# Routing rows of a mixture of experts into a region per expert, batch by batch, with gathered outputs

## The reference

```python
shared = mean over 2 shared experts of gelu(x @ sW1 + sb1) @ sW2 + sb2
gates = xf @ rW + rb                       # 8 experts, 2048 tokens
topk_vals, topk_idx = top_k(gates, 2)
topk_probs = softmax(topk_vals)
h = gelu(xf @ W1[e] + b1[e])               # 128 -> 512
y = h @ W2[e] + b2[e]                      # 512 -> 128
moe = sum over the token's two experts of prob * y
x = layernorm(x + shared + moe)
```

## Time and profile before

| | |
|---|---|
| median of 3 runs | 782.09 us (780.53 to 788.21) |
| span of the profiled execution | 786.9 us |
| PE busy | 566.9 us (72%) |
| DVE busy | 363.1 us (46%) |
| ACT busy | 338.1 us (43%) |
| POOL busy | 251.2 us (32%) |
| moved by DMA | 51.60 MB, mean 66 GB/s |
| mean granted TensorE clock | 0.824 of full speed |

### The profile page before, as it was taken

One profiled execution on the slowest core, in us unless ns is written; L12 is line 12 of the kernel. 1 busy time (PEld: TensorE's weight loads), 2 busy tenths in 40 slices (PEclk: granted clock), 3 DMA queues, 4 the chain that ended last, 5 costly groups with the idle time before them and its releaser, 6 DMA issues.

```text
span 786.9 us, 10406 instructions
## 1 busy us (share of the span) xinstructions
PE 566.9 (72%) x3665; PEld 404.0 (51%) x3665; DVE 363.1 (46%) x1067; ACT 338.1 (43%) x565; POOL 251.2 (32%) x296
## 2 busy tenths in 40 slices
PE   2654552678788869878699882996987696987770
PEld 2213431455355633656436752765874675776660
DVE  4869279616673465645624571226321240133113
ACT  1186574565737556654475140330322242322220
POOL 3204047202351254311613147113322437033231
PEclk9955665689897989987589996999878788969895
DMA  4400000395000000000000102532161402656632
GB/s 125 147 1 1 1 1 0 82 170 195 1 1 1 15 1 0 1 1 1 1 0 1 55 14 69 154 102 67 39 188 43 135 21 100 190 143 182 200 94 80
DMA packets 37763, 51.60 MB, mean 66 GB/s; under 512 B 7097, under 2 KB 27362, under 8 KB 37442
## 3 DMA queue, kind: packets, MB, share of 16 engines
q1 hardware_dynamic: 35218, 45.82, 20.9%
q0 software_dynamic: 2496, 5.15, 1.8%
HBM read 41.28 MB, written 13.86 MB: 70 GB/s over the span
## 4 chain that ended last, share of the span: by engine, by line
PE 44%; DVE 23%; POOL 7%; DMA 7%; ACT 7%; issue 7%; SPq 5%; POOLq 0%; DVEq 0%; ACTq 0%
SPq L427 5%; PE ring_s L850 4%; PE bank_d L760 4%; PE bank_o L880 3%; PE bank_m L682 3%; PE ring_s L652 3%; PE ring_u L747 3%; PE bank_o L866 3%; PE ring_s L844 2%; DMA token_pairs<-y_blk,x_blk 2%; PE bank_o L669 2%; DMA x_blk<-expert_rows 2%; POOL expert_rows L1150 2%; PE bank_r L546 2%; PE ring_u L739 2%
## 5 line engine op out<-in xcount | busy, mean ns | idle before, releaser
L958 ACT ACTIVATE probs<-ring_s 128x512 f32<-128x512 f32 (+1 forms) x192 | 95.5, 524 | 118.6 <-PE ring_s L652 116.9
L1100 POOL TENSOR_SCALAR_AFFINE_SELECT probs<-probs 128x256 f32<-128x256 f32 (+1 forms) x96 | 51.6, 570 | 178.7 <-ACT probs L964 178.7
L652 PE MATMUL ring_s<-qT,kT 64*128 64x128 bf16 (+3 forms) x256 | 64.2, 350 | 49.4 <-ACT probs L958 37.8
L1013 ACT ACTIVATE g_ring<-ring_s,w_blk 128x128 f32<-128x128 f32 x184 | 52.5, 370 | 104.4 <-PE ring_s L850 95.4
L1161 POOL DMA_INDIRECT token_pairs<-y_blk,x_blk x46 | 45.6, 991 | 143.9 <-DVE y_blk L1672 143.1
L964 ACT ACTIVATE probs<-probs 128x2560 f32<-128x2560 f32 x32 | 74.8, 2337 | 0.8
L652 PEld LDWEIGHTS ring_s<-qT,kT 64*128 64x128 bf16 x256 | 16.4, 97 | 93.4 <-ACT probs L958 58.6
L850 PE MATMUL ring_s<-xT_blk,w_blk 128*128 128x128 f32 x368 | 57.0, 305 | 4.3 <-DVE xT_blk L1665 2.6
L682 PE MATMUL bank_m<-pair_sum,oT 128*128 128x64 f32 x256 | 44.0, 327 | 22.2 <-DVE oT L1467 22.2
L1063 POOL TENSOR_TENSOR rstd<-var_eps,neg_half 128x4 f32<-128x4 f32 x24 | 24.9, 1036 | 100.5 <-DVE var_eps L1394 100.4
L850 PEld LDWEIGHTS ring_s<-xT_blk,w_blk 128*128 128x128 f32 x368 | 53.4, 222 | 6.8 <-issue 4.3
(11 more groups left out here) (356 smaller groups left out, 1076.8 us busy)
## 6 DMA issues: line engine op xcount, KB each, us to landing
w_blk<-expert_pack SPq DMA_DIRECT2D x46, 514.0 KB
expert_pack<-in_L_ffn_W SPq DMA_DIRECT2D x16, 256.0 KB
expert_rows<-blank SPq DMA_DIRECT2D x2, 1560.0 KB, 10.5
x_blk<-expert_rows SPq DMA_DIRECT2D x46, 65.0 KB
y_pair<-token_pairs SPq DMA_DIRECT2D x4, 512.0 KB
x_in<-in_x SPq DMA_DIRECT2D x4, 256.0 KB, 2.9
cosm<-in_c_cos SPq DMA_DIRECT2D x1, 1024.0 KB, 6.8
sin_fwd<-in_c_sin_fwd SPq DMA_DIRECT2D x1, 1024.0 KB, 9.4
```

Of the source, the lines that this page charges most:

```text
L652: last = mm(bank[:, c:c + w], kT[64 * r:64 * r + 64, p // 2, P * j:P * (j + 1)], qT[64 * r:64 * r + 64, p, P * j:SEQ], start=True, stop=True)
L958: f(probs[:, p % 2, BASE[n]:BASE[n] + WIDTH[n]], ring_s[k % 2][:, 0:WIDTH[n]], ACT.Tanh, scale=1.0 / (CAP * float(np.sqrt(np.float32(HD))) ...
L1013: last = f(g_ring[:, s % RING, P * n:P * (n + 1)], ring_s[s % 2][:, P * n:P * (n + 1)], ACT.Gelu, bias=w_blk[:, k % SLOTS, HID + n:HID + n ...
L1100: last = g.affine_select(out=v, in_=v, compare_op=ALU.is_ge, fill=0.0, base=0, pattern=[[0, v.shape[1]], [1, P]], channel_multiplier=-1)
```

## The change

- `rows_dram` is laid out by expert: 1024 rows for each of 8 experts in a group, and 896 rows behind them, all filled with zeros (`zero_rows`, eight rows of 512 B a partition, repeated) from SP right after the input loads.
- A row's place in its expert's region doesn't need the block table, so `rows_of(b)` follows `rank` of each batch, and `scatter(b)` writes that batch's rows straight from x2, 8 indirect DMAs of 128 rows. `copy_rows`, `x_rows` and the two extra columns go.
- The block table now also gives each block's source row (`source`), and afterwards, for each token, the rows of its two outputs in block order (`y_rows`); the weights are kept in `w_sel`.
- `load_block` reads two registers, expert and source row. b2, repeated over the partitions, is part of the pack (64 KB more a block, eight more loads at the start), its own load and the one-row matmul go, and DVE adds it at the eviction.
- SP stores block outputs in block order (`store_block`), before the load that reuses the slot; POOL has no part in the blocks. Once a group's outputs have landed, POOL gathers them per batch with 8 indirect DMAs (`fetch`), two batches ahead of their two powers, and `final` has eight multiply-adds of 128x128 in place of two adds of 128x512.

```diff
+CAPACITY = GB * SEQ
+GROUP_ROWS = NE * CAPACITY + (NE - 1) * P
+ZERO_ROWS = 8
+PACK = HID + HC + HID + D
...
+            sp.wait_ge(blank_ready, 1)
+            for g in range(GROUPS):
+                at = g * GROUP_ROWS
+                load(rows_dram[at:at + NE * CAPACITY, :].rearrange("(p n r) w -> p n (r w)", p=P, r=ZERO_ROWS),
+                     zero_rows[:, :].unsqueeze(1).broadcast_to([P, NE * CAPACITY // (P * ZERO_ROWS), ZERO_ROWS * D]), blanked)
+                load(rows_dram[at + NE * CAPACITY:at + GROUP_ROWS, :].rearrange("(p r) w -> p (r w)", p=P), zero_rows[:, 0:(NE - 1) * D], blanked)
             sp.wait_ge(kij_ready, 1)
...
+                load(pack[e, :, B2_AT:PACK], t["L0_ffn_b2"][e].partition_broadcast(P), ld_pack)
...
-            sp.wait_ge(blank_ready, 1)
-            for g in range(GROUPS):
-                load(rows_dram[g * GROUP_ROWS:(g + 1) * GROUP_ROWS, :].rearrange("(p r) w -> p (r w)", p=P),
-                     blank[:, :, :].rearrange("p r w -> p (r w)"), blanked)
...
                 if k >= SLOTS:
                     sp.wait_ge(u_down, BLOCKS[k - SLOTS] + 1)
+                    sp.wait_ge(y_ready_blk, k - SLOTS + 1)
                 e = sp.value_load(table[0:1, g, q:q + 1], min_val=0, max_val=NE - 1)
                 load(w_blk[:, k % SLOTS, :], pack_dram[bass.ds(e * P, P), :], w_landed[k % SLOTS])
-                load(b2_blk[0:1, k % SLOTS, :], t["L0_ffn_b2"][bass.ds(e, 1), :], w_landed[k % SLOTS])
-                if k >= SLOTS:
-                    sp.wait_ge(y_sent[k % SLOTS], 16 * (k // SLOTS))
-                at = g * GROUP_ROWS + q * P
-                load(x_blk[:, k % SLOTS, :], rows_dram[at:at + P, :], xs_landed[k % SLOTS])
...
+                at = sp.value_load(source[0:1, g, q:q + 1], min_val=0, max_val=GROUPS * GROUP_ROWS - P)
+                load(x_blk[:, k % SLOTS, :], rows_dram[bass.ds(at, P), :], xs_landed[k % SLOTS])
+
+            def store_block(k):
+
+                g, q = divmod(k, NB)
+                sp.wait_ge(y_ready_blk, k + 1)
+                load(y_dram[g][P * q:P * (q + 1), :], y_blk[:, k % SLOTS, :], y_sent[k % SLOTS])
...
+                for q in range(NB + SLOTS):
                     k = g * NB + q
...
+                    if q >= SLOTS:
+                        store_block(k - SLOTS)
+                    if q < NB:
+                        load_block(k)
...
-                        mm(dst, g[:, P * n:P * (n + 1)], w_blk[:, k % SLOTS, HID + HC + P * n:HID + HC + P * (n + 1)], start=(n == 0), stop=False)
-                    last = mm(dst, ones2[0:1, :], b2_blk[0:1, k % SLOTS, :], start=False, stop=True)
+                        last = mm(dst, g[:, P * n:P * (n + 1)], w_blk[:, k % SLOTS, HID + HC + P * n:HID + HC + P * (n + 1)],
+                                  start=(n == 0), stop=(n == HC - 1))
...
-                for j in range(GB * NT):
+                pool.wait_ge(blanked, 32 * (b // GB + 1))
+                pool.wait_ge(rows_ready, b + 1)
+                for j in range(NT):
                     for k in range(2):
...
+            def fetch(b):
+
+                if b % GB == 0:
+                    pool.wait_ge(y_rows_ready, b // GB + 1)
+                    for n in range(SLOTS):
+                        pool.wait_ge(y_sent[n], 16 * len(range(n, (b // GB + 1) * NB, SLOTS)))
+                if b >= 2:
+                    pool.wait_ge(pair_used, b - 1)
+                for j in range(NT):
+                    for k in range(2):
+                        g.indirect_dma_start(out=y_pair[:, b % 2, j, k, :], out_offset=None, in_=y_dram[b // GB],
+                                             in_offset=bass.IndirectOffsetOnAxis(ap=y_rows[:, k, b * NT + j:b * NT + j + 1], axis=0)).then_inc(pair_landed[b % 2], 16)
...
+            for of in range(GROUPS):
+                for b in range(GB * of, GB * (of + 1)):
+                    fetch(b)
+                for b in range(GB):
                     power()
...
+                dve.wait_ge(rank_read, b + 1)
+                rows_of(b)
                 if b % GB == GB - 1:
-                    dve.wait_ge(rank_read, b + 1)
                     block_table(b // GB)
-                    rows_of(b // GB)
...
+                one(tt(ends, ends, start_of[:, :].unsqueeze(1).broadcast_to([P, NB, NE]), ALU.mult))
+                one(v.tensor_reduce(source_of[:, :], ends, AX, ALU.add))
+                one(stt(out=source_of[:, :], in0=index[:, 0:NB], scalar=float(P), in1=source_of[:, :], op0=ALU.mult, op1=ALU.add))
+                op(ts(source[0:1, g, :], source_of[0:1, :], float(g * GROUP_ROWS), None, ALU.add))
                 ts(table[0:1, g, :], expert_of[0:1, :], float(NE - 1), None, ALU.min).then_inc(table_ready, 1)
...
-                ts(y_blk[:, k % SLOTS, :], down_bank(k)[:, 0:D],
-                   x_blk[:, k % SLOTS, D + 1:D + 2], None, ALU.mult).then_inc(y_ready_blk, 1)
+                tt(y_blk[:, k % SLOTS, :], down_bank(k)[:, 0:D], w_blk[:, k % SLOTS, B2_AT:PACK], ALU.add).then_inc(y_ready_blk, 1)
...
-                one(tt(a, a, y_pair[:, b % 2, :, 0, :], ALU.add))
-                tt(a, a, y_pair[:, b % 2, :, 1, :], ALU.add).then_inc(pair_used, 1)
+                dve.wait_ge(pair_landed[b % 2], 16 * 2 * NT * (b // 2 + 1))
+                for k in range(2):
+                    for j in range(NT):
+                        last = stt(out=a[:, j, :], in0=y_pair[:, b % 2, j, k, :], scalar=w_sel[:, k, b * NT + j:b * NT + j + 1],
+                                   in1=a[:, j, :], op0=ALU.mult, op1=ALU.add)
```

More of the change, by code:

```diff
@@ L1049, in _ @@
             op(g.memset(ones2[:, :], 1.0))
[L1050 to L1051 removed]
+            op(g.memset(zero_rows[:, :], 0.0))
+            for e in range(NE):
+                op(g.memset(expert_row[:, e:e + 1], float(e * CAPACITY)))
             then()
@@ L1131, in ff_norm @@
                 g.tensor_tensor(fa[:, :, :], fa[:, :, :], x1[:, b % 2, :, :], ALU.add).then_inc(sum_ready, 1)
-            def copy_rows(b):
-                pool.wait_ge(x2_ready, b + 1)
-                if b >= GB and b % GB == 0:
-                    pool.wait_ge(scattered[b // GB - 1], 16 * 2 * NT * GB)
-                for k in range(2):
-                    last = g.tensor_copy(x_rows[:, k, NT * (b % GB):NT * (b % GB + 1), 0:D], x2[:, b, :].rearrange("p (j d) -> p j d", j=NT))
-                last.then_inc(rows_copied, 1)
```

156 lines of the change are left out of this document (70 added, 86 removed).

## The result

The changed kernel is slower by 0.7%, not faster by 2.6%: 786.94 us (median of 19 runs, 778.93 to 803.15) against 782.39 us for the kernel before beside it (19 runs, 774.52 to 803.76). The ratio is 1.0072, 95% interval [1.0038, 1.0106], within the 1% that the prediction called no change. Some executions of either kernel take over 1.5% longer than its fastest; the ratios and intervals here leave those out, the medians don't. The prediction was 761.9 with a range of 748 to 777.

A forecast was written before the change was run, and what follows sets the result against it. No engine was full, so hand-overs between engines set the end. Terms -0.5 + 4.7 - 14.0 + 1.0 - 12.5 - 13.0 + 14.1 = -20.2 us took the median 782.09 to 761.9, range 748 to 777.

The forecast's parts named there:

- Zero fill (1): Start: the fill grows to 9.3 MB, some 34 us, hidden behind SP's 122.5 us wait for the kernel taps.
- x_in (2): Expert pack at the start: x_in of batch 2 lands 5 us earlier to 8 later; -0.5 us, upper end +8.
- Batch 0 alone (3): Batch 0's routing: eight scatters on POOL delay the power queued behind them; +4.7 us, range 0 to 10.
- Batch 1 alone (4): Batch 1's routing: only eight scatters ahead of POOL's power, PE's 14.02 us idle won; -14.0 us, gain 10.1 to 15.5.
- Batch 2 and group 0's blocks (5, 6): Batch 2's scatters and row work +1.0 us; of group 0's blocks, -5.4 near 560 to 589 and -5.0 after 605.
- stays in the sum: DVE's accumulate at 666.37, idle 16.37 us without a known releaser, left unchanged; 6 us put into the range either way.
- have POOL to themselves: Gathers of the first two batches, between scatter(3) and final(0): hidden by some 5 us, 1.264 for each that isn't.
- Batch 3: ... nothing: Batch 3's eight scatters end long before PE needs group 1, so they change nothing.
- Group 1 (6): Group 1's expert blocks: SP's issuing at 3.0 us a block becomes the limit; -13.0 us, gain 0 to 18.
- The end (7): After the last output: 16 gathers, 20.2 us, ahead of two powers, then eight chained steps; +14.1 us, range +10 to +34.
- SP's queue binds more: Rival: SP's queue or the lower clock keeps blocks at 3.5 us, nothing gained in group 1; 780 us, chance 0.13.
- DVE holds POOL up: Rival: batch 0's scatters slowed amid DVE's attention work; +2 us, 764, or +11, 773; chance 0.05.

The follow-up runs named there:

- two_batches: spread with batch 0's scatters held back and issued with batch 1's, 16 in one train; ratio 0.9928 to the kernel before.
- late_rows: spread with DVE's row numbers of batches 0 and 2 some 30 us later, their scatters in two trains of four; 755.66 us, ratio 0.962.
- late_only: The changed kernel with only the later row numbers and scatters of batches 0 and 2, gathers where the change puts them; 777.38 us, ratio 0.9817.
- bias_matmul: spread with the bias added on PE again by a one-row matmul per block and a plain copy as eviction; ratio 0.9954 to the kernel before.
- spread: The changed kernel with the 16 gathers of batches 0 and 1 issued one per block of group 1, their finals later; 768.95 us, ratio 0.9852.
- before_paused: The kernel before with a memset of some 0.94 us waited for after every fourth of group 1's 16 scatters; ratio 1.0017.
- store_on_pool: spread with group 1's 23 output stores issued by POOL as plain DMAs instead of SP; ratio 0.9858 to the kernel before.

## Why the prediction was wrong, step by step

- **Zero fill (1), x_in (2).** Right within what can be told. SP issued the fill from 24 to 42 us, its transfers kept the DMA engines busy until 55, some 30 us where 34 were taken, long before the taps; and PE had no wait for x_in. A loss of 3 us ahead of the first rank matmul would not show.
- **Batch 0 alone (3).** +4.7 predicted, +5.8 measured (+4.2 at like clock): the size is luck, the reason was wrong. The sum put it on the scatters ahead of POOL's power and counted DVE's "some 17 small ops" (15 in the trace), "about 3 us ahead of its oT copy", as a by-product. two_batches has the 5 us without a scatter; late_rows and late_only take 4.2 of them away with the scatters still in, though later. The scatters' own price is 0.6 us (the power 17.0 us behind the rank matmul without them, 17.6 with them), because the variance that the power waits for is late by DVE's work anyway.
- **Batch 1 alone (4).** Right in mechanism: -16.1 with the first five downs, -17.1 measured. The power stands 13.8 us nearer to the rank matmul, and PE's idle is gone. Taken apart it fits less well: two_batches gives the split train 10.4 us where -14.0 was taken, bias_matmul gives the bias 3.4 where 2.1 was taken, and some 3 us have no run of their own.
- **Batch 2 and group 0's blocks (5, 6).** -9.4 predicted for the stretch, -2.9 measured. "rows_of delays one xT_blk copy. +1.0" was mis-sized: late_only has 68.4 us there, 6.7 less than the changed kernel, and what it moved is the row work and the train at that point. With 68.4 the stretch is 9.6 under before, where the sum had it.
- **The accumulate of the earlier trace rows "stays in the sum", and the first two batches' gathers that "have POOL to themselves" and are "hidden" (5, 7).** This is the step that failed, by 15.1 us. I asked only whether POOL had time for the gathers. I had a row of another engine standing 16.37 us beside a train of 16 indirect DMAs, with no releaser in the trace, and did not ask what the two had to do with each other, nor what a train of 24 would do. By that row alone, a microsecond for each DMA, eight more would have been put at some 8 us; the wait grew by 12.75, from 16.37 us with 16 to 29.12 with 24. "Batch 3: ... nothing" hid a second error of the other sign: with half the scatters ahead of SP the stretch would have fallen from 33.4 to 25.5 us, as spread has it, so the gathers cost 22.9 us and the change kept 15.1 of them. The 6 us put in the range for the wait were too few, and by before_paused the old wait cost nothing as it stood.
- **Group 1 (6).** -13.0 predicted, -10.3 measured. SP's step with nothing to wait for is 2.75 us (stores at 723.54 and 726.29), under the 3.0 taken. But "SP's issuing is the new limit of a long run" was wrong: store_on_pool relieves SP and gains nothing. The transfers, which the sum had set aside at 235 GB/s "below the 270", or PE's clock set the pace.
- **The end (7).** +14.1 predicted, +13.8 measured; gathers 1.25 us apart where 1.264 was taken, the eight chained steps 2.31 us where 2.2 was. The Trainium skill's fit (page "DMA: Bandwidth & Descriptors") would have made it 2.15 us each if they waited for one another; they don't.
- **The rivals.** None of them was it. "SP's queue binds more" has the time nearest (780), but store_on_pool shows that SP's queue does not bind, and group 1 gained 10.3 us where that rival had nothing. "DVE holds POOL up" is answered the other way round: the scatters beside DVE's attention work took 0.95 to 1.23 us, while DVE's small steps beside POOL's adds took up to seven times their length. The Trainium skill ("SBUF — State Buffer", SBUF: two separate sides) names the shared DVE and POOL port as a point of contention; these rows (1.30 us where 0.19 is usual) are in line with that.

## What to carry to other kernels

Work that has an engine to itself can still cost: before a train of indirect DMAs on POOL is called hidden, look at what the other engines did beside such a train in the trace of before, and price each further DMA by it: here 1.0 us each by that row, and 1.6 us each for the eight further ones. Where such DMAs must be many and are not urgent, issue them one by one among other work, or with a pause of a microsecond between them. A wait whose releaser the trace does not know is a row to explain before it is left in a sum, and a chain of small steps on the engine that feeds the densest one belongs in that engine's idle time.

## What the runs showed of the hardware

- While POOL issues indirect DMAs 1.25 us apart without a break, ACT, DVE, PE and SP's issuing all come nearly to a stand: with 8 + 16 of them 48 us where 25.5 to 30.1 are needed with the 8 alone, 57.9 where the kernel before has 33.4 with 16 + 16. Sixteen plain DMAs of the same bytes, contiguous and over in 8.7 us, or 21 us of memsets, do nothing of the kind. A pause of 1.24 us between any two leaves 2.7 of the 22.9 us, pauses after every fourth 13.9.
- Why is open. PE and ACT go on in bursts and then stand, and SP's issues are drawn out too, so it is likely something that all of them share. An obvious candidate is that they ran out of instructions. DMA queues of the changed kernel from 640 to 674 us, columns packets, MB, share of 16 engines:

```profile
q0 software_dynamic: 768, 1.57, 15.6%
q1 hardware_dynamic: 576, 1.32, 12.9%
q8 instruction: 1, 0.02, 0.2%
```

This one packet came between 644 and 645 us, early in the train, and the next between 679 and 680. ACT went on at 653.39 and at 673.15 without one. In the second profile none came from 634 to 669 us, and ACT went on at 639.89, 651.87 and 662.47. An engine that had waited for instructions would have gone on when some arrived, so, as far as the profile records these packets, this candidate does not fit. The Trainium skill ("Runtime: NRT & Kernel Launch", Instruction fetch mechanics) has each engine fetch ahead by its own DMA queue, with a cost that is mostly hidden; these rows show nothing against that. The DMA engines themselves were far from full (under 30% of their time for the two queues above).
- DVE steps of 0.19 us took 0.66 to 1.30 us beside POOL's element-wise adds of 128x512 (two_batches; 0.92 and 1.26 in spread).
